# Attention output as two fp16 halves: six fp16 products a tile in place of two fp32 ones in the output projection

## The reference

```python
def _L1_attn_ref(x, Wq, Wk, Wv, Wo, bo):
    ...
    out = jnp.einsum('bhqk,bhkd->bhqd', attn, v)
    out = out.transpose(0, 2, 1, 3).reshape(b, s, e)
    return out @ Wo + bo
...
t = t + _L1_attn_ref(_ln_t(t), ...)
t = t + _L1_ffn_ref(_ln_t(t), ...)
```

## Time and profile before

| | |
|---|---|
| time, median of 3 runs | 1661.14 us (1660.44 to 1661.31) |
| profiled execution, its own time | 1659.74 us |
| its span, first to last instruction | 1657.7 us |
| mean granted TensorE clock | 0.996 |
| PE busy | 1586.3 us (96%) |
| DVE busy | 1188.0 us (72%) |
| ACT busy | 904.0 us (55%) |
| one image, from projection to projection | about 197.7 us |

### The profile page before, as it was taken

The page is one execution under the profiler, slowest core; times in us unless marked ns, Lnnn a source line. Parts: engine busy times, 40 slices in busy tenths (PEclk is TensorE's granted clock), DMA queues, the critical chain, the costliest instruction groups (busy, mean ns, idle before and its releaser), DMA issues.

```text
span 1657.7 us, 32908 instructions
## 1 busy us (share of the span) xinstructions
PE 1586.3 (96%) x13274; PEld 1034.4 (62%) x13274; DVE 1188.0 (72%) x2537; ACT 904.0 (55%) x1329; POOL 173.5 (10%) x247
## 2 busy tenths in 40 slices
PE   3989999999999999999999999999999999999999
PEld 1534676657665576656766567665776557765676
DVE  6687786767776776867768678676777777686644
ACT  3217654466545665466554665446654566545665
POOL 2200102001210003000020010200121000300000
PEclk9999999999999999999999999999999999999999
DMA  4202002100111002010020100200011100200000
GB/s 162 59 25 65 1 1 68 35 16 2 41 28 49 1 1 68 1 49 1 1 68 1 50 2 1 67 26 25 1 38 32 49 1 1 68 1 11 1 11 10
DMA packets 25131, 47.30 MB, mean 29 GB/s; under 512 B 7410, under 2 KB 16946, under 8 KB 23700
## 3 DMA queue, kind: packets, MB, share of 16 engines
q1 hardware_dynamic: 15728, 27.85, 6.1%
q0 software_dynamic: 6144, 9.45, 2.4%
q10 hardware_dynamic: 3108, 7.91, 1.3%
HBM read 19.82 MB, written 6.29 MB: 16 GB/s over the span
## 4 chain that ended last, share of the span: by engine, by line
PE 73%; DVE 17%; ACT 5%; issue 2%; POOL 1%; DMA 1%; SPq 0%; DVEq 0%; ACTq 0%; POOLq 0%
PE ps L440 22%; PE ps L732 18%; PE ps L677 10%; PE ps L475 6%; DVE mx L1174 4%; PE ps L618 4%; PE ps L524 3%; DVE room L1361 3%; PE ps L447 2%; ACT room L900 2%; DVE norm_stats L1015 2%; ACT room L908 2%; DVE acc L1345 1%; PE ps L511 1%; PE ps L479 1%
## 5 line engine op out<-in xcount | busy, mean ns | idle before, releaser
L900 ACT ACTIVATE room<-ps,b_sb 128x512 f32<-128x512 f32 x384 | 263.1, 685 | 438.5 <-PE ps L440 438.4
L732 PE MATMUL ps<-wout_h,room 128*128 128x192 f16 x3072 | 457.2, 246 | 0.0
L1361 DVE SCALAR_TENSOR_TENSOR room<-room 128x512 f16<-128x512 f32 x384 | 263.2, 689 | 183.0 <-ACT room L908 180.8
L732 PE MATMUL ps<-wout_l,room 128*128 128x192 f16 x1536 | 377.4, 246 | 0.0
L732 PEld LDWEIGHTS ps<-wout_h,room 128*128 128x128 f16 x3072 | 285.9, 98 | 34.0 <-issue 3.2
L880 ACT ACTIVATE room<-ps 128x1024 f32<-128x1024 f32 (+3 forms) x288 | 224.8, 811 | 141.4 <-PE ps L479 104.0
L1174 DVE TENSOR_REDUCE mx<-ps 128x2 f32<-128x1024 f32 (+3 forms) x288 | 265.8, 953 | 33.7 <-PE ps L622 21.1
L908 ACT ACTIVATE room<-room 128x512 f16<-128x512 f32 x384 | 241.9, 630 | 33.6 <-PE ps L732 0.4
L677 PE MATMUL ps<-room,v 128*64 128x512 f32 (+3 forms) x1152 | 231.7, 486 | 0.9 <-DVE o L1306 0.9
L618 PE MATMUL ps<-qk 96*128 96x512 f16 (+3 forms) x576 | 151.0, 329 | 17.4 <-DVE mx L1174 10.6
L732 PEld LDWEIGHTS ps<-wout_l,room 128*128 128x128 f16 x1536 | 150.1, 98 | 27.1
(11 more groups left out here) (203 smaller groups left out, 2317.4 us busy)
## 6 DMA issues: line engine op xcount, KB each, us to landing
xc<-x_ch SPq DMA_DIRECT2D x8, 768.0 KB, 5.8
qk<-qk_all SPq DMA_DIRECT2D x96, 64.0 KB, 2.3
qk<-qk_all POOLq DMA_DIRECT2D x96, 64.0 KB, 2.5
out<-acc ACTq DMA_DIRECT2D x16, 384.0 KB, 2.6
xt<-x_tok SPq DMA_DIRECT2D x7, 768.0 KB, 7.1
qk<-qk_all POOLq DMA_DIRECT2D x96, 32.0 KB, 2.0
qk<-qk_all SPq DMA_DIRECT2D x96, 32.0 KB, 2.3
room<-w_in SPq DMA_DIRECT2D x2, 1024.0 KB, 8.5
```

The source lines that it names most:

```text
L732: mm = pe.matmul(dst, hid[:, s, tok], w[:, n, :], start=(k == 0 and m == 0 and t % 2 == 0), stop=False, skip_group_check=True)
L900: act.activation(h32[:, i % N_H, :], ps[:, H_BANK[i], :], ACT.Gelu, scale=1 / (U_SCALE * W_SCALE), bias=b1_sb[:, n:n + 1])\
L1361: V.scalar_tensor_tensor(out=h_l[:, s, :], in0=h32[:, s, :], scalar=A_SCALE, in1=h_h[:, s, :], op0=ALU.mult, op1=ALU.subtract)\
```

## The change

The attention's output `o32` is no longer a factor of the projection. ACT copies each slot of it to fp16 (`o_h`, two activations), DVE subtracts that from `o32` and writes the rest as fp16 (`o_l`, two `tensor_tensor`), and each tile's projection is three fp16 products for each of the two slots, with weights that were split at setup into `wo_h` and `wo_l`, times 64 (`W_SCALE`). The residual's factor takes that back. The halves lie in `tmp`, which `front` uses too, so that ACT's first write there in `front` now waits for the projection of the image before (`wo_ps`) in place of `o_done`. The new piece `split` is due at 17.5 (ACT) and 18.5 (DVE) in block 0, where all other dues move by one item, and at 2 (ACT) and 3 (DVE) in block 1, where the other dues stay. At setup DVE has four more steps.

```diff
-TAIL_AT = ({"wo": 18.5, "residual": 18.5, "norm": 22.5, "turn": 25.5, "high": 26.5, "low": 26.5, "scores": 29.5,
-            "gate": 29.5, "best": 31.5},
-           {"wo": 4, "residual": 4, "norm": 6, "turn": 9, "high": 9, "low": 9, "scores": 10,
+TAIL_AT = ({"split": 17.5, "wo": 19.5, "residual": 19.5, "norm": 23.5, "turn": 26.5, "high": 27.5, "low": 27.5,
+            "scores": 30.5, "gate": 30.5, "best": 32.5},
+           {"split": 2, "wo": 4, "residual": 4, "norm": 6, "turn": 9, "high": 9, "low": 9, "scores": 10,
             "gate": 10, "best": 13})
...
+        wo_h = sb("wo_h", [P, 2, C], F16)
+        wo_l = sb("wo_l", [P, 2, C], F16)
...
+        o16 = tmp[:, 0:2 * N].bitcast(F16)
+        o_h = o16[:, 0:2 * QB].rearrange("p (c n) -> p c n", c=2)
+        o_l = o16[:, 2 * QB:4 * QB].rearrange("p (c n) -> p c n", c=2)
+        OUT_ROWS = (slice(0, P), slice(0, TAIL + 1))
...
@@ tensor, tail
-                pe.wait_ge(o_done, at(o_done, img, (b + 1) * PAIRS))
+                pe.wait_ge(o_lo, at(o_lo, img, b + 1))
                 for t in range(TB):
                     dst = ps[:, bank + t // 2, (t % 2) * C:(t % 2 + 1) * C]
                     tok = slice(t * P, (t + 1) * P)
-                    pe.matmul(dst, o32[:, 0, tok], wo32[:, 0, :], start=True, stop=False)
-                    mm = pe.matmul(dst, o32[0:TAIL + 1, 1, tok], wo32[0:TAIL + 1, 1, :], start=False, stop=True)
+                    for n, (o, w, c) in enumerate(((o_h, wo_h, 0), (o_h, wo_l, 0), (o_l, wo_h, 0),
+                                                   (o_h, wo_h, 1), (o_h, wo_l, 1), (o_l, wo_h, 1))):
+                        rows = OUT_ROWS[c]
+                        mm = pe.matmul(dst, o[rows, c, tok], w[rows, c, :], start=(n == 0), stop=(n == 5))
...
@@ scalar, front
                 if later:
-                    act.wait_ge(o_done, at(o_done, img, 0))
+                    act.wait_ge(wo_ps, at(wo_ps, img, 0))
...
@@ scalar, tail
+                yield when["split"]
+                act.wait_ge(o_done, at(o_done, img, (b + 1) * PAIRS))
+                if b or img:
+
+                    act.wait_ge(wo_ps, at(wo_ps, img, b * TB // 2))
+                for c, rows in enumerate(OUT_ROWS):
+                    ins = act.activation(o_h[rows, c, :], o32[rows, c, :], ACT.Copy)
+                ins.then_inc(o_hi, 1)
...
@@ vector, tail
+                yield when["split"] + 1
+                dve.wait_ge(o_hi, at(o_hi, img, b + 1))
+                for c, rows in enumerate(OUT_ROWS):
+                    ins = V.tensor_tensor(o_l[rows, c, :], o32[rows, c, :], o_h[rows, c, :], ALU.subtract)
+                ins.then_inc(o_lo, 1)
...
-                        scalar=1 / A_SCALE, in1=t1[:, n:n + 2, :],
+                        scalar=1 / (A_SCALE * W_SCALE), in1=t1[:, n:n + 2, :],
...
@@ vector, setup
             first.finish()
+            for c, rows in enumerate(OUT_ROWS):
+                step(V.tensor_scalar(wo_h[rows, c, :], wo32[rows, c, :], W_SCALE, None, ALU.mult))
+                step(V.scalar_tensor_tensor(out=wo_l[rows, c, :], in0=wo32[rows, c, :], scalar=W_SCALE,
+                                            in1=wo_h[rows, c, :], op0=ALU.mult, op1=ALU.subtract))
             attend(0, False)
```

More of the change, by code:

```diff
@@ L335, in build @@
         o_done = sem("o_done", NB * PAIRS)
+        o_hi = sem("o_hi", NB)
+        o_lo = sem("o_lo", NB)
         tail_step = sem("tail_step", NB * TAIL_STEPS)
```

## The result

| | before | after |
|---|---|---|
| median, us | 1660.79 (1659.69 to 1661.31) | 1682.95 (1681.13 to 1684.31) |
| profiled execution / its span, us | 1659.74 / 1657.7 | 1681.13 / 1679.1 |
| one middle image, us | 197.27 | 199.80 |

The changed kernel takes 1.0137 times as long (95% interval 1.0123 to 1.0152), 22.2 us more; forecast were 1681 us, in a range from 1671 to 1690. "One middle image" is the distance between the first products of the group variances of two successive images. From projection to projection it is the same 197.27 us in the kernel before, for images 1 to 7, and not the 197.7 given above. In nearly all kernels it agrees to 0.05 us from image to image, so that a tenth of a microsecond an image can be read from it.

The account below looks back on a forecast made before the run. PE, busy 96%, was taken as the bound, with L499 in block 1 set by an ACT-DVE chain without slack. Terms of 15.8 + 0.9 + 1.4 + 1.8 = 19.9 us led to 1681 us, range 1671 to 1690.

Parts of the forecast that it names:

- PE's own gain: Projection on PE: 24 fp16 products take 1.98 us instead of 2.65, a gain of 0.67 us a block.
- The rule on the loads: Projection: weight loads on the same rows not hidden, products 180 ns apart, 24 us more, 1705 us; rival, chance 0.02.
- Copies and subtractions: Making the halves: two ACT copies take 1.06 us start to start, two DVE subtractions 1.20 us.
- Block 1, images 0 to 6: Copies and subtractions make `gn_v` and L499 2.26 us later an image: 15.8 us in seven, up to 18.6.
- Block 1, image 7: No `front` and no L499 there, so only the later projection counts: 0.9 us (0.7 to 1.3).
- Block 0, images 1 to 7: Projection gains 0.2 us, later dues moving `uh` cost 0.4: 0.2 us slower an image, 1.4 us in seven.
- Block 0, image 0: Copies stand behind ACT's conversion of expert weights; the projection starts some 1.9 us later: 1.8 us (0.5 to 2.8).
- the clock rival: Behind block 1's new waits PE's clock falls to one half: 12.6 us more over seven images, 1693 us; chance 0.07.
- the forecast's own sign of being wrong: Profile signs against it: projection starting without a wait, `gn_v` moving less than 2 us, or clock under 1.00 behind waits.
- Setup: Four added DVE steps fall where DVE stands 5.57 us for the first pair's values: hidden, otherwise at most some 2 us.
- The four terms: Block 1 images 0 to 6, block 1 image 7, block 0 images 1 to 7, block 0 image 0: 19.9 us.
- The stretch from 62 us: Image 0 of the kernel before: PE busy 0.92 of 2 us, after which the clock stayed at 1.00, 2.4 GHz.

Follow-up runs that it names:

- the one without halves: Changed kernel with the six fp16 products and weight halves kept, the output's halves not computed and the old dues: 1655.0 us.
- The two kernels with one part each: Changed kernel with ACT's copies but no DVE subtractions, 1667.3 us; and with the subtractions but no copies, 1666.6 us (one run each).
- The kernel with the dues alone: Kernel before with only the steps of block 0's tail due one item later: 1663.8 us.
- two orders of block 1: Changed kernel, block 1 and `front` sums later: 1674.7 us, 1662.7 with block 0's halves earlier; or variances first: 1665.7, in the kernel before 1670.6.
- a third: Changed kernel with block 0's halves earlier, block 1's steps and `front`'s sums later, and `front` from `xs` on one chunk later: 1705.8 us.
- the copies alone: Changed kernel without DVE's subtractions, the low half replaced by other fp16 values: 1667.3 us (one run).
- block 0 earlier: Changed kernel with block 0's halves two items earlier and its other steps due as in the kernel before: 1672.2 us.
- The kernel with block 1 later: Changed kernel with block 1's halves and later steps and `front`'s sums one chunk later, projection, residual and norm two: 1674.7 us.

## Why the prediction was right, step by step

- **PE's own gain** (0.67 us a block): right. The 24 products take 1.99 us in block 1, 2.65 before. In block 0, 2.10 with the change to the next operands, 2.81 before. That change, 0.1 us in the prediction, measures 0.11.
- **The rule on the loads.** All loads of the 24 products use the same rows (128, or the first 65 of them) and last 95 to 101 ns, and the products start 81 to 94 ns apart, 83 in the mean, in the changed kernel at full clock as in the one without halves. The rule of the Trainium skill's page "TensorE: Matmul & The Clock Gate" (section "Part 3: Packing small matmuls — row/col tiling"), taken without the exception that it makes there for the background weight buffer, would have them about 180 ns apart (an estimate, from 82 ns and a load of 98 ns); this trace does not show it, and the measurement decides.
- **Copies and subtractions**: right. Two copies take 1.04 us from the first start to the next instruction (573.96 to 575.00; 1.06 predicted), two subtractions 1.20 (1.20).
- **Block 1, images 0 to 6**: right. Predicted were 1.53 us of wait at the projection, some 1.8 at `gn_v` and 2.26 us later an image; measured are 1.49, 1.64 and 2.27 (of them 1.03 up to the end of the projection and 1.24 at L507, by the same instructions of both traces). The 1.8 was 0.16 too much, for PE ends the projection later by as much as the 0.17 that the wait does not show; so the waits for `gn_v` add up to 11.5 us and not to the 12 to 14 forecast. The two kernels with one part each show that the sum is made of these two parts.
- **Block 1, image 7**: 1.03 against 0.9. The wait costs 1.49 and the 0.17 that idle time does not show, less the gain of 0.65.
- **Block 0, images 1 to 7**: right in sum, 0.28 against 0.2, and also in its two halves: -0.23 at the projection (-0.2) and +0.51 by the later dues (+0.4). The kernel with the dues alone has 0.53. The second half is partly luck: the forecast put all of it on `uh`, which accounts for the wait of 0.35 us, and the transposes' wait of 0.23 us was not in it.
- **Block 0, image 0**: mis-sized, 3.1 us and not 1.8 (0.5 to 2.8). The start of the projection was estimated well: PE stands 2.24 us where it stands 0.44 in the other images, so it starts 1.80 us later than there (1.9 predicted). But then the products ran at half clock, 3.74 us to the next scores and not 2.10, which the sum did not have. This 1.6 us is the clock rival in one place of the kernel, and the forecast's own sign of being wrong, a clock under 1.00 behind a wait, came true there; that it would be in all seven images was wrong.
- **Setup** was hidden as said: behind the four steps DVE still stands 4.40 us for the first pair's values, 5.57 before.

The four terms as measured are 7 x 2.27 + 1.03 + 7 x 0.28 + 3.1 = 22.0 us; the spans differ by 21.4, and the rest is the scatter of setup: `attend` starts 0.5 us earlier in the changed kernel's trace. All four came out a little above their forecast (19.9 us in sum), so that no error hid another. In the range, the low ends add up to 14.9 us and not to 15.1 (0.9 was taken for the low end of image 7, which is 0.7); the 1676 us stay.

## What to carry to other kernels

A change that takes time from the busiest engine is worth nothing at a place where another engine's chain ends last, and it costs there whatever it adds to that chain; so read the chain of each place where the edit stands, not the share of the span (DVE at 72% of the span was at 90% in the 22 us around block 1's projection). When the same edit stands in two places, cost them apart and keep it only where it has cover: block 0 alone, with its halves made two items earlier, gave 0.3%, and both blocks as first changed lost 1.4%. And an order that removes a wait has to be followed to the next step that is due on the same engine: two orders of block 1 here only moved the wait to `xs`, one of them even without any halves, and a third moved it on to `ul`, `al` and the maxima.

## What the runs showed of the hardware that I had not expected

The granted clock did not follow from the length of a wait. With the copies alone, PE stands 2.10 us for `gn_v` in each of seven images, at the same place of the same program. The stretches around it (columns as above), first in the image at 777 us, then in the next at 975:

```profile
774.00:776.00 2.00, 0.88 (x5) 0.20 (x2) 1.86 (x13) 1.14 (x3) 0.00 (x0) 1.00 0.00 0
776.00:778.00 2.00, 1.02 (x13) 1.03 (x14) 1.86 (x9) 0.33 (x1) 1.33 (x2) 1.00 0.00 0
778.00:780.00 2.00, 2.00 (x19) 1.41 (x18) 1.87 (x8) 0.57 (x1) 0.78 (x1) 1.00 0.00 0
...
972.00:974.00 2.00, 0.97 (x5) 0.24 (x3) 1.87 (x11) 1.14 (x3) 0.00 (x0) 1.00 0.00 0
974.00:976.00 2.00, 0.93 (x12) 0.94 (x13) 1.86 (x9) 0.41 (x1) 1.23 (x2) 1.00 0.00 0
976.00:977.00 1.00, 1.00 (x8) 0.59 (x7) 0.89 (x5) 0.00 (x0) 0.88 (x1) 0.77 0.00 0
977.00:978.00 1.00, 1.00 (x4) 0.29 (x2) 1.00 (x4) 0.00 (x0) 0.00 (x0) 0.50 0.02 8
```

In one of the seven the clock fell to 0.50 (1.2 GHz) behind the wait and came back at about 980 us, and that image took 199.77 us and not 198.09; in the other six it stayed at 1.00 (2.4 GHz). Likewise the waits of 1.49 us (1.55 in image 0) kept the clock in block 1 of the changed kernel, and with block 0 earlier the same wait of 1.55 us in image 0 was followed by 0.50 from about 178.5 to 182 us. There it cost nothing that shows: L507 has no wait in that image, where the six others have 1.65 us. In the changed kernel itself, besides two falls ahead of `attend` that the kernel before has too, it fell only in image 0, behind the wait of 2.24 us:

```profile
142.00:144.00 2.00, 0.51 (x6) 0.05 (x2) 0.60 (x1) 2.00 (x5) 0.00 (x0) 1.00 0.02 9
144.00:146.00 2.00, 1.25 (x9) 1.20 (x10) 2.00 (x3) 0.55 (x1) 0.00 (x0) 0.73 0.00 0
146.00:148.00 2.00, 2.00 (x15) 1.90 (x14) 1.45 (x2) 0.00 (x0) 0.00 (x0) 0.50 0.00 0
```

The kernel with block 1 later has the same wait of 2.24 us there, and the clock stays low twice as long:

```profile
146.00:148.00 2.00, 2.00 (x16) 1.90 (x16) 2.00 (x1) 0.00 (x0) 0.00 (x0) 0.57 0.00 0
148.00:150.00 2.00, 2.00 (x15) 1.39 (x14) 0.95 (x3) 0.00 (x0) 0.00 (x0) 0.50 0.03 8
150.00:152.00 2.00, 2.00 (x14) 1.24 (x12) 1.90 (x11) 1.09 (x2) 0.00 (x0) 0.50 0.00 0
```

By the same instructions of both traces this takes 1.5 us more than in the changed kernel, which had itself lost 1.6. The stretch from 62 us of the kernel before, after which the prediction saw the clock stay at 1.00, is no sure case either: behind the same instructions it fell to 0.50 at about 66 us in five of the other traces. So a wait of 1.5 to 2.2 us can cost its own length or 1.6 to 3.1 us more, and nothing in these rows tells which it will be.
